# Reordering the first batch of an attention and expert kernel: keys ahead of scores, a copy a unit sooner, another bank for the next batch's keys

## The reference, cut to what matters

```python
# x: (4, 512, 256); context: (4, 512, 256); 16 heads of 16 columns; windows of 64 rows
x = x + tanh(g_xattn) * xattn(layernorm(x), context, context)
x = x + tanh(g_ffn)   * moe(layernorm(x))

# xattn, for each batch: q, k, v = projections with W_q, W_k, W_v and biases
# window i of the queries sees the keys and values of window i-1 and, causally, of window i
sim  = einsum('bnid,bnjd->bnij', q * d**-0.5, k_of_two_windows)
out  = einsum('bnij,bnjd->bnid', softmax(where(mask, sim, lowest)), v_of_two_windows)
return out @ W_o.T + b_o
# moe: the best of 16 experts for each token, at most 160 tokens in each, gelu(x @ w1) @ w2, weighted
```

## Time and profile before

| what | value |
|---|---|
| median of 3 runs | 341.07 us |
| the profiled execution, its own time | 339.78 us |
| its span, first to last instruction | 338.0 us |
| mean granted TensorE clock | 0.985 |
| PE busy | 311.0 us (92%) |
| DVE busy | 205.1 us (61%) |
| ACT busy | 172.9 us (51%) |
| POOL busy | 149.6 us (44%) |

### The profile page before, as it was taken

How to read it: one execution, slowest core, us unless ns; L and a number is a source line. 1 busy time by engine, 2 the same in 40 slices (tenths; PEclk the granted TensorE clock), 3 DMA queues, 4 the chain that set the end, 5 groups by cost and what they waited for, 6 DMA issues and landing times.

```text
span 338.0 us, 8493 instructions
## 1 busy us (share of the span) xinstructions
PE 311.0 (92%) x2823; PEld 249.8 (74%) x2823; DVE 205.1 (61%) x980; ACT 172.9 (51%) x651; POOL 149.6 (44%) x181
## 2 busy tenths in 40 slices
PE   8868979999999899988889999999999999999990
PEld 4536846876688675767668888888888988888870
DVE  2799788999999988999972423333222333233320
ACT  2489999998999899999222111111111111111110
POOL 6389566776697746666453122111222222211122
PEclk9998999999999999999999999999999999999996
DMA  7811595119121831203054898899888888888400
GB/s 217 290 58 24 182 375 164 26 37 334 37 95 57 230 117 62 88 22 95 5 186 145 257 317 263 283 299 289 271 275 260 277 277 275 258 269 277 139 18 12
DMA packets 42070, 60.54 MB, mean 179 GB/s; under 512 B 3704, under 2 KB 32912, under 8 KB 42032
## 3 DMA queue, kind: packets, MB, share of 16 engines
q1 hardware_dynamic: 38928, 53.28, 50.1%
q0 software_dynamic: 2560, 6.25, 5.3%
q10 hardware_dynamic: 544, 0.52, 0.4%
HBM read 44.60 MB, written 14.19 MB: 174 GB/s over the span
## 4 chain that ended last, share of the span: by engine, by line
PE 62%; ACT 16%; DVE 13%; issue 5%; POOL 1%; DVEq 0%; POOLq 0%; ACTq 0%
PE bank L1637 21%; PE bank L1654 17%; ACT probs L649 12%; PE bank L1665 5%; DVE probs L850 3%; PE bank L1269 3%; PE bank L1322 3%; DVE rows L925 2%; PE bank L1280 2%; ACT q_par L623 2%; PE bank L1230 2%; PE bank L1310 2%; ACT probsT L662 2%; PE bank L1620 1%; DVE probsT L869 1%
## 5 line engine op out<-in xcount | busy, mean ns | idle before, releaser
L649 ACT ACTIVATE probs<-probs,low 128x128 f32<-128x128 f32 x256 | 99.2, 402 | 2.3 <-DVE low L850 2.3
L780 ACT ACTIVATE w_raw<-bank 128x480 f32<-128x480 f32 (+1 forms) x48 | 25.3, 527 | 122.0 <-PE bank L1637 122.0
L492 POOL TENSOR_TENSOR probs<-probs,r_total 128x512 f32<-128x512 f32 x64 | 66.3, 1049 | 29.5 <-DVE r_total L859 29.2
L1637 PE MATMUL bank<-xdT,w 128*128 128x160 f32 x512 | 75.1, 300 | 0.2 <-DVE xdT L1185 0.2
L1637 PEld LDWEIGHTS bank<-xdT,w 128*128 128x128 f32 x512 | 71.6, 190 | 1.5 <-issue 0.7
L580 POOL DMA_INDIRECT out_dram<-base,place x16 | 14.0, 878 | 115.9 <-DVE base L1206 115.9
L1654 PE MATMUL bank<-w,w_raw 128*128 128x256 f32 x256 | 62.4, 386 | 0.0
L850 DVE CUSTOM_DVE_ANT_0 probs<-bank,mask_now 128x128 f32<-128x128 f32 x256 | 57.2, 282 | 3.9 <-PE bank L1310 3.3
L1198 DVE SCALAR_TENSOR_TENSOR base<-bank,base 32x256 f32<-32x256 f32 x64 | 30.6, 478 | 47.0 <-PE bank L1665 45.3
L1654 PEld LDWEIGHTS bank<-w,w_raw 128*128 128x128 f32 x256 | 46.4, 190 | 11.5 <-issue 6.6
L649 ACT ACTIVATION_READ_ACCUMULATOR probs<-probs,low 128x1 f32 x256 | 51.8, 202 | 0.0
(11 more groups left out here) (123 smaller groups left out, 417.1 us busy)
## 6 DMA issues: line engine op xcount, KB each, us to landing
w<-in_L_ffn_w_dram SPq DMA_DIRECT2D x32, 1024.0 KB, 6.2
expert_queue<-empty_row SPq DMA_DIRECT2D x1, 5140.0 KB, 18.2
q_rows<-expert_queue SPq DMA_DIRECT2D x16, 160.0 KB, 6.1
base<-expert_queue SPq DMA_DIRECT2D x16, 129.0 KB, 5.6
ctx_rows<-in_ctx_dram SPq DMA_DIRECT2D x4, 512.0 KB, 9.1
out_dram<-rows SPq DMA_DIRECT2D x4, 512.0 KB, 7.2
x_all<-in_x_dram SPq DMA_DIRECT2D x3, 512.0 KB, 7.2
v_shift<-v SPq DMA_DIRECT2D x12, 128.0 KB, 2.3
```

Source lines behind the costliest of these rows:

```text
L492: pool.tensor_tensor(probs[:, i % NP_], probs[:, i % NP_], r_total[:, i % NP_].unsqueeze(2).to_broadcast([P, PAIRS, 2 * WINDOW]), ALU.mult ...
L649: last = act.activation(probs[:, i % NP_, j], probs[:, i % NP_, j], ACT.Exp, scale=-1.0, bias=low[:, i % NP_, j:j + 1], accum_out=total[:, ...
L780: act.activation(hidden[:, ms[0]:ms[-1] + 1, :], ps_hidden[m][:, 0:n].rearrange("p (m c) -> p m c", c=CAP), ACT.Gelu_apprx_tanh).then_inc( ...
L1637: last = pe.matmul(ps_hidden[m][:, c * CAP:(c + 1) * CAP], w1_sb[i % 2][:, k, f * P:(f + 1) * P], xdT[i % 2][:, k], start=(k == 0), stop=( ...
```

## The change

In the first batch alone (`b == 0`, or `first`):

1. PE: `k_of(0, 1)` moves ahead of `scores(0, 0)`, and the turning of W_v (`wT_of(2, ...)`) moves behind `scores(0, 0)`. ACT: `take_k(0, 1)` moves from behind `exp(0, 1)` to directly behind `take_q(0, 0)`, ahead of `take_wT(2, ...)`, the tanh of the gates and all exponentials.
2. ACT: `take_xnT(1, 0)` moves from behind `exp(0, 7)` to ahead of it.
3. `k_of(1, 0)` is written into `ps_wide` where it was written into `ps_misc`. PE waits before it for `take_att(0, 0)` (the semaphore `att_taken` at 1) where it waited for `take_q(1, 0)`, and before `attend(0, 1)` it waits for `take_k(1, 0)`. ACT: `take_k(1, 0)` moves from behind `exp(0, 13)` to ahead of `exp(0, 12)`.

```diff
             take_k(0, 0, bank[3])
             take_q(0, 0, bank[2])
+            take_k(0, 1, ps_wide)
             take_wT(2, 3, bank[4])
             act.wait_ge(small_in, 4 * 16)
             act.activation(tanh_g[:], gates[:], ACT.Tanh).then_inc(tanh_ready, 1)
             for b in range(LAST):
                 exp(b, 0)
                 exp(b, 1)
-                take_k(b, 1, ps_wide)
+                if b > 0:
+                    take_k(b, 1, ps_wide)
                 take_q(b, 1, ps_misc)
...
                 exp(b, 6)
+                if b == 0:
+                    take_xnT(b + 1, 0, ps_misc)
                 exp(b, 7)
-                take_xnT(b + 1, 0, ps_misc)
+                if b > 0:
+                    take_xnT(b + 1, 0, ps_misc)
                 take_probsT(b, 3)
...
                 take_q(b + 1, 0, ps_misc)
                 take_probsT(b, 7)
+                if b == 0:
+                    take_k(b + 1, 0, ps_wide)
                 exp(b, 12)
                 exp_logits(b - 1)
                 exp(b, 13)
-                take_k(b + 1, 0, ps_misc)
+                if b > 0:
+                    take_k(b + 1, 0, ps_misc)
                 take_probsT(b, 9)
...
             k_of(0, 0, bank[3])
             q_of(0, 0, bank[2])
+            pe.wait_ge(xnT_taken, 1)
+            k_of(0, 1, ps_wide)
+            pe.wait_ge(pads_ready, 2)
+            scores(0, 0)
             pe.wait_ge(wT_taken[0], 1)
             wT_of(2, bank[4])
-            pe.wait_ge(pads_ready, 2)
-            scores(0, 0)
-            k_of(0, 1, ps_wide)
             q_of(0, 1, ps_misc)
...
-                pe.wait_ge(q_taken, value(b + 1, 2, 1))
-                k_of(b + 1, 0, ps_misc)
+                if first:
+
+                    pe.wait_ge(att_taken, value(b, 4, 1))
+                else:
+                    pe.wait_ge(q_taken, value(b + 1, 2, 1))
+                k_of(b + 1, 0, ps_wide if first else ps_misc)
                 probsT_of(b, 8)
                 probsT_of(b, 9)
                 if first:
-                    pe.wait_ge(att_taken, value(b, 4, 1))
+                    pe.wait_ge(k_taken, value(b + 1, 2, 1))
                 else:
                     pe.wait_ge(logits_taken, value(b - 1, 1, 1))
                 attend(b, 1)
```

## The result

The changed kernel takes 340.10 us (median of 20 runs, 339.74 to 341.37) where the kernel before takes 340.85 (20 runs, 340.58 to 342.02). The ratio is 0.9976, with a 95% interval of 0.9967 to 0.9986: 0.8 us faster, less than the 0.3% beyond which the prediction would have called it faster. 340.2 was forecast.

The account below looks back on a forecast made before the run. The prediction took ACT's stream up to 67 us as the bound. Its terms, -0.53 + 0.24 - 0.60 = -0.89 us, taken off the median of 341.07, gave 340.2 us, with a range of 339.2 to 341.4.

Parts of the forecast that it names:

- The bound: ACT's stream from 18.31 to 67.26 us sets the end; gains to PE or DVE alone are slack.
- Part 1, -0.53: Second group's keys copied in ACT's idle 1.87 us: third unit 0.53 us sooner, 0.04 allowed for small delays.
- The copy of the turned rows, +0.24: ACT, asking for batch 1's turned x rows a unit sooner, waits 0.24 us for PE's transposes; copy at 31.17.
- The context stall, -0.60: ACT's wait for PE before the context rows' copy at 36.12 disappears: 0.60 us gained, or 0.50 counting only idle.
- Part 3, 0: Batch 1's first keys in the values' bank: PE gains up to 1.8 us as slack, ACT neither stalls nor gains.
- Sum: The terms on ACT's stream up to 67 us total -0.89 us, or -0.79 with the smaller idle.
- Rival 1: All ACT's standing time goes, including 0.54 us before batch 1's queries' copy: ceiling 1.71 us, 339.4 us; chance 0.17.
- Rival 2: Gain eaten by ACT waiting 0.5 us or more at the turned x rows' copy: 340.8 us; chance 0.15.
- Rival 3: A DVE chain from 67 us, which ACT only grazes, sets the end: 341.0 us; chance 0.10.
- Rival 4: Longer PE pause puts the low clock on the turned x rows, stalling ACT 2.6 us: 342.8 us; chance 0.08.

Follow-up runs that it names:

- e3: Kernel before with only batch 1's first keys moved to the values' bank and copied ahead of unit 12; 340.91 against 340.74 us, ratio 1.0009.
- e9: Changed kernel with unit 7's turned probabilities copied ahead of batch 1's queries and 12 idle matmuls in PE's pause; 338.58 us against 340.01 for before.
- e12: Kernel before with only the second group's keys moved ahead of the first scores, plus 12 idle matmuls in PE's pause; 339.45 against 340.01 us, ratio 0.9981.
- e6: Kernel before, unedited, run once more for a second trace; one execution, 341.63 us.
- e10: Changed kernel, unedited, run again in the third series; 339.46 us against 340.01 for before, ratio 0.9988.
- e2: Kernel before with only the copy of batch 1's turned x rows moved one unit sooner; 340.45 against 340.74 us, ratio 0.9991.
- e11: Kernel before with 8 idle matmuls added in PE's pause of 2.69 us; 341.35 against 340.01 us, ratio 1.0035.
- e5: Changed kernel, unedited, run again in the second series; 340.96 us against 341.54 for before, ratio 0.9983.
- e8: Changed kernel with 12 idle matmuls added in PE's pause of 3.46 us; 340.68 us against 341.54 for before, ratio 0.9977.
- e4: Changed kernel without the move of batch 1's first keys to the values' bank; 340.32 us against 340.74 for before, ratio 0.9979.
- e7: Changed kernel with, in the first batch, unit 7's turned probabilities copied before batch 1's queries and its first keys behind unit 12; 340.46 against before's 341.54 us.
- e1: Kernel before with only the second group's keys computed and copied ahead of the first scores and exponentials; 340.28 against 340.74 us, ratio 0.9993.

## Why the prediction was right

**The bound.** Right. ACT's stream up to 67 us set the end. The shift of ACT at the queries' copy (0.77), at the x1 norm (0.78) and at the dispatch (0.79) is one and the same, and e3, which gives slack to PE and DVE only, moves none of them. The direct test is e9: an edit that moves a copy of 0.48 us (43.96 to 44.44 in the changed kernel) into ACT's stall makes the x1 norm 0.49 sooner.

**Part 1, -0.53.** -0.49 (third unit), and -0.50 at the x1 norm in e12. The first exponential was 0.10 late, where 0.04 was allowed: W_v's copy started at 17.82 instead of 17.7. The first scores were late too, 16.02 for 15.95, so that DVE's row minimum would have held the exponential until 18.39 (17.42 + 0.97) had W_v not done it.

**The copy of the turned rows, +0.24.** This is the term that was too small. The copy was reckoned at 31.17 and came at 31.31, so +0.33 from the third unit's shift of -0.49 (18.60 - 1.54 - 0.49 = 16.57, measured 16.90). DVE's part was right (`low_of(0, 4)` at 24.93 for 24.88, last row minimum at 28.20 for 28.18), but PE's third scores started at 28.64, not 28.5: from the end of DVE's last instruction, 28.48, to the scores it took 0.16 us, where I gave 0.04. The rows came 0.14 later than reckoned and ACT itself 0.05 later: 0.24 + 0.14 - 0.05 = 0.33.

The prediction also measured from a place that the low clock had set, the 28.99 of the earlier trace rows. In the trace of before the second scores took 1.42 us, and DVE's last row minimum behind them stands 0.22 later than in e6, counted from the first copy of queries. Then PE itself came late: its transposes ran from 28.02 up to the scores without a pause, while DVE had been done since 28.65. Where the clock stayed at 1.00, PE stands and waits for DVE. First e6 (before), then e10 (after):

```profile
28.91 1.17 PE L1310 MATMUL bank<-kT,q_par 32*128 32x128 f32 x32 [1.16 <-DVE low L850]
```

```profile
28.77 1.17 PE L1318 MATMUL bank<-kT,q_par 32*128 32x128 f32 x32 [1.20 <-DVE low L858]
```

Counted from the first copy of queries, the third scores start at 14.58 in the first trace of before and in e2 (both at the low clock), at 14.17 or 14.18 in e6, e3 and e11 (clock 1.00), and at 14.23 in all five traces of after, e5, e8, e9 and e10, at either clock. So the change moves ACT by 0.49 and does not move the third scores at all: the 0.35 between the two first traces is what the low clock had cost PE in before, where nobody waited for it. This is where the stall of 0.33 comes from: part 1 brings ACT to the turned rows sooner and not the rows. The stall of 0.19 in e2, in turn, is the low clock's: from the third scores to the copy it takes 2.67 us in e2 as in after, so with the scores at 14.18 the rows would be there at 16.85, ahead of ACT at 17.06 (18.60 - 1.54). Part 2 alone would then gain some 0.6 us, an estimate that no run shows. At the x1 norm the parts alone, as measured, sum to 0.92 us (0.50 + 0.41 + 0.01) and the whole is 0.78: the difference is the 0.14 between the two stalls, 0.33 and 0.19.

**The context stall, -0.60.** Right: 31.31 to 35.36 is dense, and from the copy's place to here ACT gains 0.60 (-0.16 at the one, -0.76 at the other). Of the two values that I weighed, 0.50 of idle and 0.60 with the overlap, the latter holds.

**Part 3, 0.** Right: no stall at 44.44, and no gain. PE's wait of 1.54 became one of 0.70 for DVE's copy of unit 6, as named.

**Sum.** -0.49 + 0.33 - 0.60 = -0.76, forecast -0.89, ratio of the runs -0.82 us (-0.48 to -1.12). That the forecast of 340.2 lies within 0.1 of the measured 340.10 is in part luck: the gain by medians was 0.75, 0.14 less than reckoned, and the base 340.85, 0.22 less than the 341.07 that it was taken off.

**The rivals.** Rival 1 (more is recovered) did not come by itself: the stall before 42.62 stayed at 0.53; e9 shows that it takes an edit of ACT's order. Its reason, that PE gets earlier by a better clock, fails as well: e10 has the clock at 1.00 and the same copy at 16.90. Rival 2 was partly so (0.33 instead of 0.24). Rival 3 falls: only the two spans spoke for it, and their equality came from the hand-over. Rival 4 was right in its kind and wrong in its place: in no trace does the low stretch fall on the turned rows. In e4 and e7, the two traces at a mean clock of 0.981, it lasts from ahead of the second scores into the transposes behind `v_of(0, 0)`, and delays the turned rows by 1.24 and 1.31 us through them. By medians, executions at 0.982 or less are longer than the others of their kernel by about 1 us in after, e1 and e4, 0.2 to 0.4 in e5 and e7, and 1.1 in e10 (340.3 for 339.1).

Whether the longer pause makes such executions more frequent is not settled. They are 20 of 74 for kernels with the pause of 3.46 us and no idle matmuls (after, e1, e4, e5, e7, e10), 11 of 120 for those with 2.69 us (before in the three series, e2, e3), none of 35 with 12 idle matmuls. That none of the 35 is among them speaks for the pause. But within the 2.69 us the kernel before has 6 of 96 and e2 and e3 together 5 of 24, close to the 20 of 74, though e3's edit acts only behind 40 us. And of the 20 executions of before that were timed beside the changed kernel six took 341.73 to 342.02 us, the other 14 at most 341.34; their clocks were not recorded. If these were low-clock executions, before had more of them there than the changed kernel, which had four of 20. The mean clock is also a rough sign, since the traces have another low stretch behind 330 us, where PE has no matmul left, which costs nothing. If the pause is the cause, these counts make it a payback of some 0.2 us on average, (0.27 - 0.09) x 1.1; the prediction had such a cost as a rival but not in its sum. The Trainium skill ("TensorE: Matmul & The Clock Gate", Part 1) has the monitor run freely of the kernel's start; these traces agree: the kernel before has the low stretch in its first trace and not in e6, the changed kernel in its first trace and not in e10.

## What to carry to other kernels

Where one in-order engine is dense, each of its idle stretches is a place for an instruction that another step of its stream needs later; count the gain from its own stream, and what other engines win as nothing until a trace shows it waited for. Compare two traces place by place, from a common early event, before comparing spans: here 0.8 us of gain was hidden by a pause that both kernels have. Ask of each place in a trace what set it: the third scores of before had been held by PE's low clock, and their move in the next trace looked like a part of the gain and was none. Moving work ahead of a wait lengthens the pause behind it, here on TensorE from 2.69 to 3.46 us; look at many executions, with their clocks, before calling that free.

## What was not expected of the hardware

- The pause of DVE at the hand-over has three levels, 0.36, 1.0 to 1.1 and 1.86 us, constant over the four kernels traced in a series and changing between the series (two of them on the same chip). Its cause was not found. The copy waits for nothing but the semaphore of PE's last dispatch matmul; it starts 0.04 us behind that matmul's end at the lowest level (179.71, 179.75), and 0.76 (after) and 1.56 us (e5) behind it at the others.
- With 12 idle matmuls in the longer pause none of 35 executions had a mean clock of 0.982 or less; with 8 of them in the pause of the kernel before, 8 of 12 executions took about 1.2 us or more longer than the median of before. They are no safe addition without many runs.
- The second scores, 32 matmuls of 128 columns, took 1.17 us at a clock of 1.00, and 1.42 (before), 1.58 (after), 1.89 (e1) and 2.09 us (e4) as the low stretch began later or earlier in them, or ahead of them.
